# Ten products of ones with a zeroed buffer placed in TensorE's waits at the start of a one-core vision transformer kernel

## The reference

```python
h = tok(x)                       # 16x16 patches -> 36 tokens + a class token, width 256, plus positions
h = layernorm(h + attention(h))  # 16 heads of 64, with contextual position terms
h = layernorm(h + moe(h))        # 8 experts, the best 2 of each token, and a shared gated MLP
```

```python
proj = jnp.einsum('bnd,ed->bne', patches, W) + b
out = jnp.concatenate([cls, proj], axis=1) + pos_embed
```

## Time and profile before

| | us |
|---|---|
| median of 3 runs | 804.93 |
| lowest and highest of them | 804.77, 805.79 |
| the profiled execution, its own time | 805.93 |
| its span, first to last instruction | 804.2 |
| TensorE matmul busy | 742.1 |
| TensorE weight loads busy | 604.0 |
| VectorE busy | 541.2 |
| ScalarE busy | 394.5 |
| GpSimd busy | 160.1 |

### The profile page before, as it was taken

The page is one execution under the profiler, slowest core; times in us unless marked ns, Lnnn a source line. Parts: engine busy times, 40 slices in busy tenths (PEclk is TensorE's granted clock), DMA queues, the critical chain, the costliest instruction groups (busy, mean ns, idle before and its releaser), DMA issues.

```text
span 804.2 us, 13635 instructions
## 1 busy us (share of the span) xinstructions
PE 742.1 (92%) x4569; PEld 604.0 (75%) x4570; DVE 541.2 (67%) x1134; ACT 394.5 (49%) x778; POOL 160.1 (20%) x200
## 2 busy tenths in 40 slices
PE   5988999999999999999999979789798999999990
PEld 5867797979797979889797948667585666666880
DVE  0069897989898988889897988653642334334673
ACT  2365857575657576675847556111012333333254
POOL 3000000000000000000000000037704666664132
PEclk9999999999999999999999989599899999999996
DMA  8921001010101010101000042020001222221611
GB/s 304 306 101 34 1 24 44 23 44 23 44 23 44 18 49 0 54 2 27 7 23 13 24 145 75 26 24 2 0 2 53 82 78 76 82 76 38 241 57 66
DMA packets 28302, 47.35 MB, mean 59 GB/s; under 512 B 4793, under 2 KB 19107, under 8 KB 28274
## 3 DMA queue, kind: packets, MB, share of 16 engines
q1 hardware_dynamic: 22802, 37.24, 14.3%
q0 software_dynamic: 5472, 9.76, 3.9%
HBM read 35.57 MB, written 13.24 MB: 61 GB/s over the span
## 4 chain that ended last, share of the span: by engine, by line
issue 64%; PE 29%; DVE 3%; DMA 2%; ACT 1%; POOL 1%; POOLq 0%; SPq 0%; DVEq 0%
PE ps_S L985 9%; PE ps_S L922 8%; PE ps_S L1003 5%; PE ps_S L937 4%; DMA down_sb<-in_x_dram 2%; PE ps_S L995 1%; PE ps_X L970 1%; POOL down_sb L560 0%; PE ps_S L825 0%; DVE wkv_sb L1698 0%; DVE wkv_sb L1695 0%; DVE tl L1606 0%; DVE wkv_sb L1584 0%; ACT kT L1138 0%; POOL rs L566 0%
## 5 line engine op out<-in xcount | busy, mean ns | idle before, releaser
L566 POOL TENSOR_TENSOR rs<-ve,neg_half 111x2 f32<-111x2 f32 x11 | 12.4, 1132 | 496.0 <-DVE ve L1433 496.0
L737 PE MATMUL ps_X<-wkv_sb,hT 128*111 128x512 f32 (+1 forms) x176 | 85.7, 619 | 7.9 <-ACT v_sb L1108 7.4
L1352 DVE COPY_PREDICATED table<-bit,table 111x112 f32<-111x112 int16 (+6 forms) x110 | 76.2, 693 | 11.4 <-DVE table L1352 0.2
L985 PE MATMUL ps_S<-gu_sb,attnT 128*128 x176 | 82.9, 593 | 0.5 <-ACT attnT L1229 0.5
L1059 ACT COPY simS<-ps_S 32x666 f32<-32x666 f32 (+3 forms) x105 | 74.2, 706 | 13.6 <-DVE table L1409 10.7
L1670 DVE COPY attnT<-ps_S 128x256 f32<-128x256 f32 x44 | 18.7, 424 | 77.6 <-PE ps_S L1003 77.6
L678 PE MATMUL ps_S<-hT,wq_sb 128*128 128x222 f32 (+1 forms) x352 | 66.2, 345 | 0.0
L737 PEld LDWEIGHTS ps_X<-wkv_sb,hT 128*111 128x111 f32 (+1 forms) x176 | 27.9, 174 | 50.7 <-issue 30.2
L678 PEld LDWEIGHTS ps_S<-hT,wq_sb 128*128 128x128 f32 x352 | 63.5, 189 | 0.1
L774 PE MATMUL ps_X<-oT,wout_sb 128*128 128x222 f32 x320 | 61.9, 350 | 0.0
L774 PEld LDWEIGHTS ps_X<-oT,wout_sb 128*128 128x128 f32 x320 | 60.1, 189 | 0.2 <-issue 0.2
(11 more groups left out here) (209 smaller groups left out, 1440.6 us busy)
## 6 DMA issues: line engine op xcount, KB each, us to landing
down_sb<-in_x_dram SPq DMA_DIRECT2D x10, 648.0 KB
gu_sb<-y_d SPq DMA_DIRECT2D x8, 512.0 KB, 7.9
h_d<-hT SPq DMA_DIRECT2D x11, 222.0 KB, 2.5
kept<-h_d SPq DMA_DIRECT2D x11, 222.0 KB, 2.6
h_d<-h SPq DMA_DIRECT2D x10, 222.0 KB
wkv_sb<-in_L_attn_Wkv_dram SPq DMA_DIRECT2D x2, 1024.0 KB, 10.2
gu_sb<-in_L_ffn_gate_w_dram SPq DMA_DIRECT2D x2, 1024.0 KB, 11.2
gu_sb<-in_L_ffn_up_w_dram SPq DMA_DIRECT2D x2, 1024.0 KB, 12.1
```

The costliest lines, as they stand in the source:

```text
L737: mm = nc.tensor.matmul(X[:r, 1 - s], hT[:, k].rearrange("p b t -> p (b t)")[:, a * ROWS:a * ROWS + r], wkv_sb[:, k, INNER + 512 * s:INNER ...
L985: mm = nc.tensor.matmul(S[:, i], xgT[:, i, k], gu_sb[:, bass.ds(e, 1), k].rearrange("p o j f -> p (o j f)"), start=(k == 0), stop=(k == KE ...
L1352: A.did(V.copy_predicated(near[:, :, :, 0:SL - d], by_side(bit[:, n], r)[:, :, :, 0:SL - d], near[:, :, :, d:SL]))
```

## The change

A helper `warm(n)` issues n matmuls: the stationary operand is `ones` (128x128), the moving operand 256 columns of the zeroed `gate`, and the result goes to bank 3 of `S`, where nobody reads it. Ten of them are issued: four ahead of everything (behind waits for the first five constants and for `zeroed`), three between the transposes of the patch weights and the wait for the small loads, one between `patches(0)` and the waits ahead of `embed(0)`, and two between `embed(0)` and the waits ahead of `keys(0)`. Nothing is removed or moved.

```diff
+            def warm(n):
+
+                for _ in range(n):
+                    nc.tensor.matmul(S[:, 3, :CHUNK], ones[:, :], gate[:, :7].rearrange("p h t -> p (h t)")[:, :CHUNK],
+                                     start=True, stop=True)
+
+            pe.wait_ge(consts, 5)
+            pe.wait_ge(zeroed, 1)
+            warm(4)
             pe.wait_ge(w_tok, 16)
             pe.wait_ge(consts, N_CONSTS)
             for s in range(3):
...
                 mm.then_inc(setup_t, 1)
+            warm(3)
             pe.wait_ge(w_small, 96)
...
             pe.wait_ge(setup_sb, 1)
             patches(0)
+            warm(1)
             pe.wait_ge(setup_sb, 3)
             embed(0)
+            warm(2)
             pe.wait_ge(tables, N_TABLES)
             pe.wait_ge(zeroed, 1)
             keys(0)
```

## The result

| | before | changed |
|---|---|---|
| median, first measurement (7 runs each) | 805.01 | 798.59 |
| lowest and highest of them | 804.77, 805.94 | 796.65, 801.78 |
| profiled execution, own time | 805.93 | 798.03 |
| its span | 804.2 | 796.3 |

The ratio is 0.9932, 95% interval 0.9909 to 0.9955: 0.7% faster. The forecast was 803.4 with 801.5 to 805.4, so the direction was right and the size far off. All times are in us.

A forecast was written before the change was run, and what follows sets the result against it. PE was taken as the bound nearly throughout, its early work at 1.2 GHz. Median 804.93 less 1.46 gave 803.5, the profiled execution 802.6 to 804.4; it said 803.4, own range 802.7 to 804.3, 8-in-10 range 801.5 to 805.4.

The forecast's parts named there:

- The gain's term: First embedding: clock rise at 14.8 to 16.7 in place of 17.9 to 19.8 us, gaining 1.46 us.
- I count the gain in full: After `keys(0)`: everything moves ahead with it, with 5 us of room before the output weights, so the early gain reaches the end.
- Slow early work: First patches and embedding: run at 1.2 GHz, costing about 1 and 3 us, the only time the products can win back.
- The cost of a product: All ten places: 0.42 us each at the lower clock, 0.21 at the full, hidden in waits; direct cost 0, at worst 0.4.
- Work of 4.2 to 6.1 us stood before a rise: PE's clock, from four places in the trace: it rises after 4.2 to 6.1 us of unbroken work.
- rival A: Start: three products bring the rise before the first embedding, gaining 3.8 us, time 801.6; chance 0.22.
- The gap of 0.70: PE idle ahead of `embed(0)`: made earlier transposes not help; one product shrinks it to about 0.3, so unbroken work starts at 10.61.
- rival C: PE's waits elsewhere: the earlier start adds one clock fall costing 1.7 us, first embedding gains nothing, time 806.6; chance 0.08.
- The spread: Whole kernel: a run can be told from no change from about 0.2%, 1.6 us.

The follow-up runs named there:

- e13: Kernel before, without the ten products, plus 24 products of constants in three late PE waits; median 798.25, ratio 0.9913.
- e2: Changed kernel, unedited, run for a second profile; ratio 0.9954 to the kernel before.
- e15: Changed kernel, unedited, run once more for further runs and a profile; ratio 0.9934 to the kernel before.
- e9: Kernel before, unedited, run for one more profile and more runs; ratio 0.9992 to the kernel before.
- e12: Changed kernel keeping only the one product between `patches(0)` and `embed(0)`; ratio 0.9965 to the kernel before.
- e5: Same edit as e13, in an earlier job where the kernel before took 824.55; ratio 0.9981.
- e6: Changed kernel plus the 24 late products of e5, in the same job as e5; ratio 0.9938 to the kernel before.
- e14: Repeat of e6, early and late products together, in a job without the long wait; median 795.58, ratio 0.9892.
- e16: As e14, with ten in place of six products ahead of the last group's weight transposes; median 793.65, ratio 0.9858.
- e11: Changed kernel with eight products in place of two ahead of the first keys; ratio 0.9974 to the kernel before, mean 801.7.
- e7: Changed kernel with transposes of ones for the products: five ahead of the patch-weight transposes, eight behind, no others; ratio 0.9962 to the kernel before.

## Why the prediction was wrong in size

Two steps failed. The gain's term was mis-sized: it placed the rise inside the first embedding and gave 1.46, and the changed profiles show the clock up before `patches(0)` and a gain of 2.0 to 2.3 at the keys. And "I count the gain in full" put everything behind the keys at nothing, while the rest after the keys differed by 5.9 between executions of one program; that, more than the first step, carried the first measurement out of the range, since 2.3 alone would have given 802.7. The direction was right, and for the keys the reason too; that the first measurement came out as large as 6.4 is in part chance.

**Slow early work.** Right for the profile that it read: patches and embedding ran at 1.2 GHz, 2.42 and most of 7.60. That only this could be won is not borne out, since the waits far behind the start hold falls that cost time too (e13).

**The cost of a product.** Mis-sized by two: 0.42 for each record at the lower clock, two records for each product, so 0.85. The first four took 3.4 in the first profile and 3.7 in e2, not 1.7, and the transposes of the patch weights started at 5.7 to 6.0, against 5.3 to 5.7 in the three profiles of before. Whether the products held them back is not shown: in the eight profiles in which PE stood idle ahead of them, the load let them start anywhere from 5.2 to 6.3. In three of the four changed profiles the longer row of work brought the clock up before the transposes ran (1.47 to 1.53 in place of 2.82; in e15 they took 2.64). The other products lay in their waits. Even the one ahead of the embedding did where it ran at the lower clock: the embedding began 0.70 behind the end of `patches(0)` in the first changed profile (13.04 to 13.74), as before.

**"Work of 4.2 to 6.1 us stood before a rise."** This bound failed, and with it the chance of 0.22 for rival A. In e9 no more than 2.8 us of transposes stood before a rise, and in all four profiles of the changed kernel the clock was up before `patches(0)`, with the embedding in 4.74 us in three of them, as A had it. The early gain of A, 3.8, lies within what the four profiles with the same rest show at the keys: from 21.50 - 19.24 = 2.3 to 22.68 - 18.68 = 4.0. Over all profiles (means of three of before and four of changed) it is 21.8 - 19.5 = 2.3; the mean is smaller because the kernel before too is sometimes lucky, which the one profile couldn't show.

**The gap of 0.70.** The forecast's mechanism was real: e12 against e9 has it alone, and it gives 1.66 at the keys, where 1.46 was forecast. That the numbers are so near is partly luck: in this pair the clock had been up and fell during `patches(0)`, while the forecast had it low from the start, and in three of four changed profiles no fall is recorded there at all.

**"I count the gain in full" and nothing besides.** The first pairs did move with the keys: in the first changed profile PE's wait near 63 begins its next work 1.99 earlier, the last group's 2.06. What the prediction left out is that the rest varies by 5.9 between executions of one and the same program with the places at which late waits bring a fall of the clock (rival C in the other direction). The first measurement, 6.4, holds some of that. Of the pooled 3.9 (with about 0.8 either way from the scatter of the runs), 2.3 to 2.6 are at the keys (with e5, e6, e13, e14 and e16, whose early parts are the same, the means are 22.1 and 19.5). Whether the last 1.3 to 1.6 is chance, or whether the changed kernel meets good late places more often, stays open: the profiles are too few, and e11 did not decide it. The runs point both ways: 15 of 112 of before lie below 800 and 6 of 37 of the changed kernel below 797.7, which is the same share 2.3 lower, but the medians, 804.5 and 799.75, are 4.8 apart.

**The spread** of before was taken from three runs within 1.0; 112 runs span 9.0.

## What to carry to other kernels

TensorE's waits can cost twice in this kernel: the wait, and the work behind it at half clock. Unread products in a wait that another engine or a load ends anyway cost little or nothing here and brought part of the second cost back; look for such places at every long wait of the kernel, above all where short transposes, or matmuls of a few columns, stand around it, and not only at its start. Count records, not calls (an fp32 matmul is two), and leave the products a little shorter than the wait. A gain that rests on the clock has to be measured over dozens of runs, or between profiles whose clock rows agree.

## What was not expected of the hardware

- Transposes alone brought the clock up (e7: patches in 1.33 after 5.7 us of nothing else; e9: 1.42 after 2.8 us), while matmuls of 8 columns did not hold it: in the changed kernel they begin at 494.68, the mean clock is 0.68 over 495 to 500 and 0.50 over 500 to 505, with PE busy 5.00 and 4.90 of 5.00 us.

```profile
494.68 3.39 PE L825 MATMUL ps_X<-rw_sb,tokT 128*128 128x8 f32 x24
...
495.00:500.00 5.00, 5.00 (x33) 5.00 (x33) 4.33 (x8) 1.19 (x3) 0.00 (x0) 0.68 0.00 0
```

- Products of ones with zeros bring the clock up too: with four of them in front, the first transposes took 1.47 to 1.65 in six of nine profiles, from 5.7 to 6.0 us on, and 1.86 to 2.64 in the other three; in the seven profiles in which nothing stands ahead of these transposes they took 2.82.
- The same program meets the falls of the clock at different places: 798.1 to 807.2 over 112 runs of before.
- A stretch at half clock is free where PE isn't what is waited for. In the first profile the clock was at 0.50 after 64 us, in the changed kernel it was not, and PE's lead grew there from 1.99 to 3.56 (68.22 less 64.66); by 470 us it was 2.1 again. The changed kernel waits at 70.20 for ACT:

```profile
64.66 1.76 PE L763 MATMUL ps_S<-attnT,v_sb 111*64 111x111 f32 x32
...
67.51 1.69 PE L678 MATMUL ps_S<-hT,wq_sb 128*128 128x222 f32 x8
70.20 2.15 PE L678 MATMUL ps_S<-hT,wq_sb 128*128 128x222 f32 x10 [1.00 <-ACT patT L1056]
```
